# Cross-attention and a low-rank feed-forward block: weights laid out by partition on the host, loads in another order, the first two tiles in an order of their own

## The reference

```
z  = layernorm(x)
q  = z @ Wq + bq ; k = ctx @ Wk + bk ; v = ctx @ Wv + bv        # 16 heads of 32
p  = softmax(clip(q k^T / sqrt(32), -10000, 10000))              # over 77 keys
x  = x + (p v) @ Wo + bo
z2 = layernorm(x)
x  = x + gelu((z2 @ U1) @ V1 + b1) @ U2 @ V2 + b2                # 512 -> 128 -> 2048 -> 128 -> 512
```

## Time and profile before

| | |
|---|---|
| three runs | 592.86, 595.11, 596.40 us (median 595.11) |
| the profiled execution | 592.9 us, span of the trace 591.1 us |
| PE busy | 558.3 us (94%) |
| DVE busy | 487.5 us (82%) |
| POOL busy | 365.7 us (62%) |
| ACT busy | 305.8 us (52%) |
| mean granted TensorE clock | 0.99 |
| HBM read, written | 32.49 MB, 16.78 MB |

### The profile page before, as it was taken

The page is one execution under the profiler, slowest core; times in us unless marked ns, Lnnn a source line. Parts: engine busy times, 40 slices in busy tenths (PEclk is TensorE's granted clock), DMA queues, the critical chain, the costliest instruction groups (busy, mean ns, idle before and its releaser), DMA issues.

```text
span 591.1 us, 12005 instructions
## 1 busy us (share of the span) xinstructions
PE 558.3 (94%) x4807; PEld 465.6 (79%) x4807; DVE 487.5 (82%) x702; ACT 305.8 (52%) x505; POOL 365.7 (62%) x282
## 2 busy tenths in 40 slices
PE   6986998999999999999987997999999999999996
PEld 6675887888889888898875776888888888888884
DVE  3499987898889988898679995797979797978675
ACT  1435344444454444544464634675757575757562
POOL 1558676757677677767667544666666666565561
PEclk9999999999999999999999997999999999999999
DMA  8523064132312322222320413012121212101012
GB/s 269 175 57 109 21 198 129 68 108 90 109 55 72 108 92 72 74 89 72 127 73 21 156 57 142 2 55 89 53 90 55 89 54 89 55 18 54 18 54 89
DMA packets 27764, 50.36 MB, mean 85 GB/s; under 512 B 2955, under 2 KB 4669, under 8 KB 27581
## 3 DMA queue, kind: packets, MB, share of 16 engines
q1 hardware_dynamic: 27229, 48.80, 24.3%
q10 hardware_dynamic: 480, 0.80, 0.5%
HBM read 32.49 MB, written 16.78 MB: 83 GB/s over the span
## 4 chain that ended last, share of the span: by engine, by line
PE 78%; DVE 6%; DMA 5%; POOL 4%; issue 3%; ACT 2%; SPq 2%; POOLq 0%; DVEq 0%; ACTq 0%
PE bank L924 46%; PE ps_s L924 15%; PE bank L998 5%; PE bank L1014 4%; PE ps_s L972 4%; DMA ss<-in_L_xattn_Wv 2%; PE bank L1039 2%; PE bank L946 2%; POOL ss L380 2%; POOL ss L388 1%; DMA fw<-y_between 1%; DVE ssum L721 1%; DMA xs<-in_x 1%; POOL wqo_r L371 1%; DVE z L653 1%
## 5 line engine op out<-in xcount | busy, mean ns | idle before, releaser
L452 POOL TENSOR_TENSOR hs_r<-ss,hs_r 128x512 fp32r<-128x512 f32 x63 | 90.4, 1434 | 92.8 <-ACT hs_r L622 92.2
L601 ACT ACTIVATE ss<-ps_s,bias_c 128x512 f32<-128x512 f32 x128 | 88.0, 689 | 69.1 <-PE ps_s L924 65.9
L924 PE MATMUL ps_s<-p1t_r,v_r 128*128 128x512 f32 x384 | 113.5, 405 | 0.3 <-DVE p1t_r L772 0.3
L924 PE MATMUL bank<-hs_r,u_r 128*128 128x512 f32 x384 | 110.4, 397 | 0.7 <-DVE hs_r L783 0.7
L380 POOL TENSOR_TENSOR ss<-ss,smax 128x1232 f32<-128x1232 f32 x32 | 75.0, 2343 | 53.5 <-DVE smax L716 53.5
L924 PE MATMUL bank<-zt_r,wqo_r 128*128 128x256 f32 x768 | 99.2, 285 | 2.3 <-DVE zt_r L661 2.3
L924 PE MATMUL bank<-wqo_r,ot_r 128*128 128x512 f32 x384 | 97.7, 403 | 0.7 <-DVE ot_r L729 0.5
L924 PEld LDWEIGHTS bank<-zt_r,wqo_r 128*128 128x128 f32 x768 | 92.5, 188 | 4.8 <-DVE zt_r L661 2.6
L924 PEld LDWEIGHTS bank<-hs_r,u_r 128*128 128x128 f32 x384 | 72.9, 190 | 18.2 <-DVE hs_r L783 1.1
L388 POOL TENSOR_TENSOR ss<-ss,rsum 128x1024 f32<-128x1024 f32 x32 | 61.5, 1922 | 39.9 <-DVE rsum L723 39.7
L924 PEld LDWEIGHTS bank<-wqo_r,ot_r 128*128 128x128 f32 x384 | 69.9, 188 | 16.4 <-DVE ot_r L729 0.9
(11 more groups left out here) (89 smaller groups left out, 826.6 us busy)
## 6 DMA issues: line engine op xcount, KB each, us to landing
xs<-in_x SPq DMA_DIRECT2D x64, 256.0 KB, 3.3
y_between<-xs SPq DMA_DIRECT2D x32, 256.0 KB, 2.0
xs<-y_between SPq DMA_DIRECT2D x4, 1024.0 KB, 5.9
fw<-y_between SPq DMA_DIRECT2D x4, 1024.0 KB, 5.5
out<-xs SPq DMA_DIRECT2D x16, 256.0 KB, 2.0
out<-fw SPq DMA_DIRECT2D x16, 256.0 KB, 2.0
ss<-in_L_xattn_Wq SPq DMA_DIRECT2D x2, 512.0 KB, 10.4
xs<-in_L_xattn_Wo SPq DMA_DIRECT2D x1, 1024.0 KB, 11.2
```

The costliest lines, as they stand in the source:

```text
L452: pool.tensor_tensor(hs[:, c % 4, 1, :], hg[:, c % 4, :], hs[:, c % 4, 0, :].bitcast(F32), ALU.subtract)\
L601: act.activation(hg[:, c % 4, :], ps_s[:, c % 4, :], ACT.Gelu_apprx_tanh, bias=b1_c[:, c:c + 1]).then_inc(h_gelu, 1)
L924: mm = pe.matmul(ps, lhs(a), rhs(c), start=first and i == 0, stop=last and i == len(PASSES) - 1)
```

## The change

The host now hands over arrays in another layout (`layouts`): each weight as 128 rows, one per partition, with everything that the partition gets in one run; Wq as two such halves; the context already transposed, in one array with the three biases that are needed by partition. With that the transposes and copies of context and biases go away.

SP's first loads are now: x of tile 0, context with biases, Wk, the halves of Wq, x of tile 1, Wv, Wo, x of tiles 2 and 3. The broadcast of bv is issued by ScalarE behind its copies of Wq, the broadcast of bo by SP behind `v_sum`, ahead of the copies that place V. Wk and Wv lie in other buffers.

The work of tiles 0 and 1 is written out on TensorE and ScalarE (`first_tiles`) and reordered on VectorE (`first_blocks`). V is made behind the first scores. What tiles 2 to 15 and the feed-forward part compute, and in which order, stays. The host's arrays are prepared outside the time measured.

The core of the diff:

```diff
@@ SP
-            sp.dma_start(ctx_f, ctx.rearrange("b k c -> k b c")).then_inc(in_ctx, 16)
             load_x(0, 0)
-            sp.dma_start(wk_f, wk.rearrange("(k p) n -> p k n", p=P)).then_inc(in_wk, 16)
+            sp.dma_start(once[:, UB * D - KC * B * KV:], ctx_bias).then_inc(in_ctx, 16)
+            sp.dma_start(wk_f, wk).then_inc(in_wk, 16)
             for half in range(2):
-                sp.dma_start(wq_half(wq_f, half),
-                             wq_half(wq.rearrange("(k p) n -> p k n", p=P), half)).then_inc(in_wq[half], 16)
-            sp.dma_start(wv_f, wv.rearrange("(k p) n -> p k n", p=P)).then_inc(in_wv, 16)
+                sp.dma_start(wq_f[half], wq[half]).then_inc(in_wq[half], 16)
             load_x(0, 1)
-            sp.dma_start(wo_f, wo.rearrange("(k p) n -> p k n", p=P)).then_inc(in_wo, 16)
+            sp.dma_start(wv_f, wv).then_inc(in_wv, 16)
+            sp.dma_start(wo_f, wo).then_inc(in_wo, 16)
             load_x(1, 0)
             load_x(1, 1)
...
+            sp.wait_ge(wo_lo, 1)
+            load_xb(0, 0)
             sp.wait_ge(v_copied, 2)
+            sp.dma_start(bias_row[:, :], bo.partition_broadcast(P)).then_inc(in_bo, 16)
             sp.wait_ge(zeroed, 1)
...
-                sp.dma_start(u2_f, u2.rearrange("(k p) n -> p k n", p=P)).then_inc(in_ffn, 16)
-                sp.dma_start(u1_f, u1.rearrange("(k p) n -> p k n", p=P)).then_inc(in_ffn, 16)
+                sp.dma_start(u2_f, u2).then_inc(in_ffn, 16)
+                sp.dma_start(u1_f, u1).then_inc(in_ffn, 16)
@@ POOL
+                    if is_block(0, j, b):
+                        rstd_of(1, 0)
+                    if is_block(1, j, b):
+                        rstd_of(1, 1)
                     if there(NA, j, b, -1):
                         normalise(*shift(j, b, -1), 1)
-                    if is_block(1, j, b):
-                        rstd_of(1, 1)
...
-                    if is_block(0, j, b):
-                        rstd_of(1, 0)
-                        normalise(0, 0, 0)
                     if there(NA, j, b, 0):
                         subtract_max(j, b, 1)
-                        if not is_block(0, j, b):
-                            normalise(j, b, 0)
+                        normalise(j, b, 0)
@@ ACT
+            turned_z(0, 0)
             for half in range(2):
                 act.wait_ge(in_wq[half], 16)
-                act.activation(wq_half(wq_r[:, 0, :, :], half), wq_half(wq_f, half), ACT.Copy).then_inc(wq_hi, 1)
-                if half == 0:
-                    turned_z(0, 0)
-            act.wait_ge(bias_ready, 1)
+                act.activation(wq_half(wq_r[:, 0, :, :], half), wq_f[half], ACT.Copy).then_inc(wq_hi, 1)
+            act.dma_start(bias_row[:, :], bv.partition_broadcast(P)).then_inc(in_bv, 16)
+            act.wait_ge(in_ctx, 16)
             q_copy(0, 0, 0)
             act.wait_ge(in_wo, 16)
...
+            def first_tiles():
+
+                exponent(0, 0, 0)
+                q_copy(0, 1, 0)
+                exponent(0, 0, 1)
+                q_copy(0, 1, 1)
+                turned_z(1, 0)
+                copy_probs(0, 0, 0, (0, 1))
+                q_copy(1, 0, 0)
+                copy_probs(0, 0, 0, (2,))
+                copy_probs(0, 0, 1, (0, 1))
+                exponent(0, 1, 0)
+                q_copy(1, 0, 1)
+                copy_probs(0, 0, 1, (2,))
+                turned_z(1, 1)
+                exponent(0, 1, 1)
+                heads_high(0, 0)
@@ DVE
             norm_z(0, 1)
-            dve.wait_ge(in_bv, 16)
-            v_sum(0)
-            v_sum(1)
-
-            turned_z(0, 1)
+            norm_stats(1, 0, 0)
+            norm_stats(1, 0, 1)
...
                 clip(0, 0, 0)
                 maxima(0, 0, 0)
-                norm_stats(1, 0, 0)
-                norm_stats(1, 0, 1)
+                turned_z(0, 1)
+                dve.wait_ge(in_bv, 16)
+                v_sum(0)
                 clip(0, 0, 1)
+                maxima(0, 0, 1)
                 norm_z(1, 0)
                 sums(0, 0, 0)
-                maxima(0, 0, 1)
+                v_sum(1)
+                norm_stats(1, 1, 0)
+                norm_stats(1, 1, 1)
                 turned_z(1, 0)
+                sums(0, 0, 1)
                 clip(0, 1, 0)
-                norm_stats(1, 1, 0)
-                sums(0, 0, 1)
                 maxima(0, 1, 0)
-                norm_stats(1, 1, 1)
+                norm_z(1, 1)
                 clip(0, 1, 1)
-                norm_z(1, 1)
                 maxima(0, 1, 1)
                 sums(0, 1, 0)
+                norm_stats(2, 0, 0)
                 turned_z(1, 1)
-                norm_stats(2, 0, 0)
+                heads_low(0, 0)
+                sums(0, 1, 1)
                 norm_stats(2, 0, 1)
-                sums(0, 1, 1)
-                heads_low(0, 0)
@@ PE
+            keep_warm(32)
+            turn_z(0, 0)
...
             pe.wait_ge(wq_lo, 1)
             project_q(0, 0, 0)
-            v_product(1)
             pe.wait_ge(wq_lo_pool, 1)
             project_q(0, 0, 1)
             turn_z(0, 1)
...
+            def first_tiles():
+
+                scores(0, 0, 0)
+                pe.wait_ge(in_wv, 16)
+                v_product(0)
+                scores(0, 0, 1)
+                project_q(0, 1, 0)
+                v_product(1)
+                project_q(0, 1, 1)
+                turn_z(1, 0)
+                scores(0, 1, 0)
+                turn_probs(0, 0, 0, (0, 1))
+                project_q(1, 0, 0)
+                turn_probs(0, 0, 0, (2,))
+                scores(0, 1, 1)
+                turn_probs(0, 0, 1, (0, 1))
+                project_q(1, 0, 1)
+                turn_probs(0, 0, 1, (2,))
+                turn_z(1, 1)
+                pe.wait_ge(v_placed, 16 * (2 + 2 * GH))
+                weigh_values(0, 0)
```

More of the change, by code:

```diff
@@ L69, in pairs, with xattn_ffn @@
         body(j)
-def xattn_ffn(nc, x, ctx, wq, bq, wk, bk, wv, bv, wo, bo, u1, v1, b1, u2, v2, b2, out):
+def xattn_ffn(nc, x, ctx_bias, wq, wk, wv, wo, bv, bo, u1, v1, u2, v2, b2, out):
     x_t = x.rearrange("b (t p) d -> (b t) p d", p=P)
@@ L311, in body @@
                             sp.dma_start(y_t[row, :, :], xb[:, k, :]).then_inc(y_out[k], 16)
-                    if there(NA, j, b, 0):
-                        for u in range(2):
-                            k = 2 * b + u
-                            row = held(tile_row(j, b, u))
-                            until(sp, y_out[k], 16 * j)
-                            sp.dma_start(xb[:, k, :], x_t[row, :, :]).then_inc(in_xb[k], 16)
+                    if there(NA, j, b, 0) and not is_block(0, j, b):
+                        load_xb(j, b)
             pairs(NA, body)
@@ L465, in _ @@
         def _(act):
-            for row, v in ((0, bq), (G, bk), (2 * G, b1)):
-                n = v.shape[0] // P
-                act.dma_start(bias_f[row:row + n, :], v.rearrange("(g p) -> g p", p=P)).then_inc(in_bias, 16)
-            act.dma_start(bias_row[:, :], bv.partition_broadcast(P)).then_inc(in_bv, 16)
             def turned_z(j, b):
@@ L680, in _ @@
             norm_z(0, 0)
+            turned_z(0, 0)
             dve.wait_ge(wq_hi, 1)
-            dve.tensor_tensor(wq_half(wq_r[:, 1, :, :], 0), wq_half(wq_f, 0),
+            dve.tensor_tensor(wq_half(wq_r[:, 1, :, :], 0), wq_f[0],
                               wq_half(wq_r[:, 0, :, :], 0).bitcast(F32), ALU.subtract).then_inc(wq_lo, 1)
-            turned_z(0, 0)
             dve.wait_ge(k_full, 1)
-            dve.wait_ge(bias_ready, 1)
+            dve.wait_ge(in_ctx, 16)
             for g in range(G):
@@ L1066, in _, with project_k @@
             pe.wait_ge(const_ready, 4)
[L1067 to L1081 removed]
+            keep_warm(32)
+            turn_z(0, 0)
+            def project_k(g):
                 for k in range(KC):
@@ L1086, in _ @@
                                      start=k == 0, stop=k == KC - 1)
+                return last
+            pe.wait_ge(in_ctx, 16)
+            pe.wait_ge(in_wk, 16)
+            for g in range(G):
+                last = project_k(g)
             last.then_inc(k_full, 1)
-            turn_z(0, 0)
-            pe.wait_ge(in_wv, 16)
-            v_product(0)
             pe.wait_ge(wq_lo, 1)
             project_q(0, 0, 0)
-            v_product(1)
             pe.wait_ge(wq_lo_pool, 1)
@@ L1203, in _, with layouts @@
                 body2(j)
-_NAMES = ["x", "ctx_768", "L0_xattn_Wq", "L0_xattn_bq", "L0_xattn_Wk", "L0_xattn_bk", "L0_xattn_Wv",
-          "L0_xattn_bv", "L0_xattn_Wo", "L0_xattn_bo", "L0_ffn_U1", "L0_ffn_V1", "L0_ffn_b1",
-          "L0_ffn_U2", "L0_ffn_V2", "L0_ffn_b2"]
+def layouts(inputs):
+    import numpy as np
+    at = lambda name: np.asarray(inputs[name])
+    rows = lambda w: w.reshape(-1, P, w.shape[1]).transpose(1, 0, 2)
+    yield "x", at("x")
+    ctx_t = at("ctx_768").transpose(2, 0, 1).reshape(KC, P, B * KV).transpose(1, 0, 2).reshape(P, KC * B * KV)
```

(16 more changed lines are left out.)

64 lines of the change are left out of this document (24 added, 40 removed).

## The result

| | runs | median | ratio to before (95% interval) |
|---|---|---|---|
| changed kernel, first comparison | 582.40 to 585.96, 4 runs | 584.14 us | 0.9853 (0.9819 to 0.9888) |
| the kernel before beside it | 590.92 to 596.40, 4 runs | 593.99 us | |
| changed kernel, compared again | 583.85 to 588.57, 7 runs | 587.44 us | 0.9909 (0.9873 to 0.9945) |
| the kernel before beside it | 589.49 to 596.21, 12 runs | 592.38 us | |

Faster, by 9.9 us between the medians of the first comparison and 4.9 us between those of the second; neither interval contains 1. Over both, the median of the 11 runs of the changed kernel is 585.96 and that of the 16 runs of before 592.66, so 6.7 us apart.

The account below looks back on a forecast made before the run. TensorE alone bounds 102 to 285 us, so an earlier entry shifts everything after it. 3.8 us at the start plus 0.8 at the wait for x made 4.6, from 595.1 to 590.5 us; range 585.8 to 595.0.

Parts of the forecast that it names:

- So Wo lands at 20.15 again.: Start: Wo lands as late as before, so first scores start at 23.5, 5.2 us earlier.
- Rival 2: Loads gain more: Wo 1.7 us earlier, wait for x gone, 2.0 more; total 8.3, to 586.8 us; chance 0.15.
- The worst case of the query product: Start: with the old landings the query product ends at 22.0, just inside wo_hi's end at 22.06.
- Early loads of Wk and Wq therefore buy nothing beyond this point: Start: loading Wk and Wq sooner brings no gain, since wo_hi, ending at 22.06, decides the first scores.
- From the first scores to weigh_values: Tile 0: VectorE decides, list 1.4 us longer, norm_z 2.93 twice; weigh_values at 54.0, 3.8 us earlier.
- So I take the full clock.: After weigh_values of tile 0: TensorE at full clock, scores of tile 2 at 55.9, 5.2 us earlier.
- rival 1: TensorE's clock falls again near weigh_values of tile 0, costing 1.4 us, to 591.9; chance 0.15.
- VectorE gives part of that back.: Tiles 2 and 3: VectorE's 2.5 us more and an unchanged 13.3 put weigh_values of tile 1 at 74.1, 3.8 earlier.
- V's placing: Copies placing V, last issued near 48.1, land in time; as a rival, late landing gives 598.4 us, chance 0.06.
- The wait for x: 0.8.: Load of x behind the feed-forward weights: longer runs save 0.8 us, bounds nothing and 2.8.
- Rival 3: The 512-byte runs of the feed-forward weights cost nothing; only 3.8 us remain, to 591.3; chance 0.12.
- After that ... the shift stays.: Behind weigh_values of tile 1: VectorE has 18 us of slack in 183, so the 3.8 us gain lasts.

Follow-up runs that it names:

- a1: Changed kernel with the broadcast of bv issued first of all by ScalarE, as before; 586.72 us, ratio 0.9901.
- b2: Kernel before with only the broadcast of bv moved behind ScalarE's copies of Wq; 590.64 us, ratio 0.9971.
- a3: Changed kernel with Wk, Wv and Wo read in runs of 2 KB and Wq of 1 KB, as before; 586.72 us, ratio 0.9905.
- c1: Changed kernel with norm_z of tile 2 ahead of the second maxima of tile 0 on VectorE; 584.07 us, ratio 0.9867.
- c2: Changed kernel with 24 unused transposes in TensorE's gap ahead of weigh_values of tile 0; 582.59 us, ratio 0.9855.
- d1: Changed kernel with x of tile 6 before feed-forward weights, norm_z of tile 3 earlier, 12 unused transposes in the start gap, later first-feed-forward-block statistics; 575.85 us, ratio 0.9730.
- a2: Changed kernel with feed-forward weights U1 and U2 read in runs of 512 bytes as before; 586.78 us, ratio 0.9907.
- b1: Kernel before with only the feed-forward weights U1 and U2 laid out by partition; 591.09 us, ratio 0.9980.
- c3: Changed kernel with 20 unused transposes in TensorE's gap near 351 us, in the first feed-forward block; 584.86 us, ratio 0.9873.

## Why the prediction was wrong, step by step

- **"So Wo lands at 20.15 again."** This is the step that failed first. It rested on the bytes ahead of Wo being the same, took the rate of before for given, and had no term for the instant of issue. Wo landed at 17.65 and 16.82, 11.2 and 10.9 us behind its issue as before (11.2), but issued 2.5 and 3.1 us earlier. By a1, b2 and a3 either of two things brings most of that: the broadcast left the first microseconds, or the runs became longer. At the first scores, 2.3 to 3.0 us more than forecast. Rival 2 had this in part, with 1.7 us, and the chance of 0.15 was too small: the earlier trace rows showed 213 beside 379, and I took the hole for a cost that moves with the broadcast.
- **The worst case of the query product.** It ended at 19.6, the same instant as wo_hi (19.57), so both limits moved together, and "Early loads of Wk and Wq therefore buy nothing beyond this point" was wrong: in the second profile the product ended last, at 18.92, with wo_hi at 18.74, and in a1 it alone decided.
- **From the first scores to weigh_values.** Right as a size: 28.5 us from the first clip, forecast 29.2. Only half right as a mechanism: c1 shows that up to 36.5 TensorE sets as late a limit, and that VectorE decides alone only from there; c2 and d1 confirm VectorE as the releaser of weigh_values. norm_z at 2.93 twice was right.
- **"So I take the full clock."** Wrong; rival 1, to which I gave 0.15, happened in both profiles. Of the 4 us of gaps that I had counted, 3.7 did stand in one piece ahead of weigh_values. The fall cost 2.5 and 1.7 us up to weigh_values of tile 1, by c2, where the rival had priced 1.4, the longer weigh_values alone.
- **"VectorE gives part of that back."** Wrong. I carried 13.3 us from before as if it were fixed work. It held a norm_z of 2.93 beside GpSimd; in the later position this took 1.31, so that the 13.3 became 11.7, and VectorE finished at 70.6, ahead of TensorE. 72.08 minus 21.19 is 50.9 where I had 50.6, but only because the clock took what VectorE did not: in c2, without the fall, it is 48.4. Two errors cancelled, by luck.
- **V's placing** never released weigh_values, nor did GpSimd: as forecast. The last of its copies was issued by 45.1, not near 48.1.
- **The wait for x: 0.8.** Too small in the first profile (1.64), too large in the second (0.46); the means put the layout at about 1. The term was a fair size. Rival 3, that runs of 512 bytes cost nothing, has the means against it, but the scatter is larger than the effect.
- **"After that ... the shift stays."** The instructions did; the clock did not. Behind the last weigh_values the first profile was 2.6 us shorter than before and the second 1.3. I had looked for the clock only where the change works. Before's profile happened to hold one of the two longest falls in that gap (251.4; a2 has 251.3), the first profile of after none.

In sum, against the forecast of 4.6 up to the scores of tile 4, for the first and the second profile: 2.3 and 3.0 more at the first scores, 0.8 and 0.8 more from there to weigh_values of tile 0, 1.1 and 0.3 less up to weigh_values of tile 1, 0.9 more and 0.3 less up to the scores of tile 4. That makes 7.5 and 7.8. The other 2.4 us of the first profile are the clock behind it. The second comparison, 4.9, is near my 4.6 by luck; its marks show the 7.8. Its profiled execution, 583.85, was one of its two short ones. The five long ones had a granted clock of 0.984 to 0.988 instead of 0.994, so longer falls of the clock are shown for them, and d1's calm agrees; in which gaps they fell is open, as only the profiled execution has a timeline.

## What to carry to other kernels

When loads are reordered, the rate of the old start is no constant: ask what made the slow stretch, and give the case that it goes a full chance. Two causes of one loss can overlap: here the removal of either brought most of what both bring, so their prices don't add up. A wait that TensorE has anyway can cost twice, once as a gap and once in the half clock that may follow; that second part comes and goes from run to run, so look through the whole trace for such gaps, and at the granted clock of every run, before comparing medians. An earlier engine is worth only as much as the next wait lets through: fix the waits in the order in which they release TensorE, and together.

## What the runs showed of the hardware

- A broadcast of one row of 2 KB to 128 partitions, issued first beside loads in runs of 1 and 2 KB, came with 184 and 213 GB/s over 4 us (b1, before); without it 254 and 272 (a3, b2), beside longer runs 356 (a1). The window alone proves little: the changed kernel's own start had 250 to 350.
- The load of Wo, 1 MB, took 10.9 to 11.2 us from issue to landing in before and in both profiles of the changed kernel; what moved was its issue, from 8.95 to 6.47 and 5.87. The issue of U1 and U2 held SP for up to 3.7 to 4.7 us in one instruction with runs of 512 bytes (before, b2, a2), and for 1.0 to 2.3 in the nine profiles with one run per partition.
- Behind some gaps of TensorE the granted clock was 1.2 GHz for some 3 to 10 us, in most executions but not in all of the same code. It fell behind the gap of 3.7 us in the start in 8 of 8 profiles, in or behind the feed-forward gap of 3.1 to 3.5 us in 10 of 12, behind the wait for x where it was 2.3 us or more in 1 of 7. With the gaps filled or removed (c2 at 50 us, c3 at 354, d1 at both) it stayed at 2.4 GHz there.
- VectorE's norm_z, a pair of 1.00 us, took 0.99 and 1.00 in the moved positions of c1 and d1 and 2.93 behind the maxima that start GpSimd's subtraction. In the first profile of the changed kernel the pair runs from 29.82 to 32.75 and this subtraction from 29.99 to 32.47, so the pair ends just behind it. By the Trainium skill (SBUF — State Buffer, SBUF: two separate sides) VectorE's two-port operations and GpSimd's exclude each other for a whole instruction; these numbers agree.
